# Group means of twelve chains by a round trip through DRAM and a sum on VectorE, in place of a product on TensorE

## The chip, the core and the metric

The kernel runs on one core of one Trainium2 chip. The metric is the time of one execution in microseconds (us) on the device; lower is better. The engines have short names in every row of the profile: PE is TensorE (PEld its weight loads), DVE is VectorE, ACT is ScalarE, POOL is GpSimd, SP is SyncE, which here only issues DMAs.

## What is computed

Sixteen images of 128 channels by 32x32 pixels pass through two convolution layers, each ahead of a group norm and with a residual sum. Cut to what matters:

```python
def _gn(v, G=32, eps=1e-05):          # 32 groups of 4 channels
    g = v.reshape(B_, G, C_ // G, H_, W_)
    m = jnp.mean(g, axis=(2, 3, 4), keepdims=True)
    s = jnp.var(g, axis=(2, 3, 4), keepdims=True)
    return ((g - m) / jnp.sqrt(s + eps)).reshape(v.shape)

def L0(x):                            # 4 experts, mixed per image
    routing = sigmoid(mean(x, (2, 3)) @ w_route.T + b_route)
    y = conv3x3(x, w_experts)         # 128 -> 4 * 128 channels
    out = einsum('beohw,be->bohw', y, routing)
    return silu(out * inv + shift)

x = x + L0(_gn(x))
x = x + conv3x3(_gn(x), sign(W))      # L1
```

The change concerns only the mean `m` of the two group norms: the mean over four neighbouring channels of the channels' own means.

## The kernel before

The 128 channels lie on the 128 partitions, and an image is a tile `X` of 128x1024. The kernel handles one image per **iteration** `t` of a software pipeline. In iteration `t` TensorE does the first convolution of image `t` (lines 439: `pb`, `pa`, `pe_`, with kernels `U`/`UM` mixed for this image by ACT line 704 and DVE line 932), then the second convolution of image `t-1` (line 474: a high and a low half, `hi` and `lo`, `pc<-hi,ws` and `pc<-lo,ws`, 18 products each). Each engine has its own written-out program; the order of its instructions is the order of the calls in the code, and semaphores are the only link between engines. Nothing is scheduled by a planner.

Group norms are done in **chains**, one chain `c` an iteration, `c = t + 2`. A chain handles two columns at once: column `IN`, the first norm of image `c`, and column `MID`, the second norm of image `c - LAG` (`LAG = 3`, so image `t-1`). The steps of a chain, with their lines:

- `nm[:, c, :]`, the two negated means of each channel, scaled: ACT line 584 (`mean_mid`, from the sum that the silu of line 732 leaves in `ysum`) and ACT line 572 (`mean_in`, `junk_mean<-X`, whose result is written by the READ_ACCUMULATOR after it).
- **the group means** `gnm`: PE line 405 (`group_means`), a product of `nm` (two columns) with the matrix `gsum`, into the PSUM bank `ps`.
- the squares of each channel's distance from its group's mean: ACT line 635 (`squares`, written to `dev2`; the profile shows it as `dev<-ps,nm`), `deviation` (line 651), `add_variance` (line 645, writes `spread`).
- the group variances: PE line 410 (`group_vars`), then ACT line 663 (`ve`), POOL line 352 (`power`, `rstd<-ve,nhalf`: the reciprocal root), ACT line 668 (`nbias`, reads `gnm` again), and ACT lines 747, 754, 686, which write `hi`, `hn` and `xn` from the normalised images.

Around this, within iteration `t` on VectorE: `all_rows(t+1)` (line 963, `e_rows`), `inner_rows(t+1)` (972, `f_rows`), `transform(t+1)` (980 to 990, `V`), one third of the mix of kernels for `t+1` (932), then the inverse transform of image `t` (997 to 1023, it waits for `pa` and ends in `y`), `low_part(t-1)` (1044, `lo<-hn,hi`), the rest of the mix with `pool_routes` (911) between, and the kernels' rows (941 to 955).

The residual sum of the first layer, `X<-y`, is an accumulating DMA of 512 KB issued by POOL (line 356) when silu is done; ACT line 592 (`junk_mid`) waits for it. SP issues the loads of `x` and, image by image as these residual sums land, the store of `X` to `out` (line 334, 512 KB):

```python
            for i in range(B - LATE):
                wait_h(sp, i)
                sp.dma_start(out_v[i, :, :], img(i)).then_inc(h_stored[i], 16)
```

POOL adds the second layer's result to `out` by another accumulating DMA (line 361), once that store is done.

Of the kernel before, what the change touches and what calls it, by code (L numbers as in the profile page):

```python
# [7 lines left out]
F32 = mybir.dt.float32  # L8
# [8 lines left out]
GSIZE = 4  # L17
# [39 lines left out]
def build(nc, x, w_experts, w_sign, params, out):  # L57
# [6 lines left out]
    with ExitStack() as ctx:  # L64
        def sb(name, shape, dt=F32):
            return ctx.enter_context(nc.sbuf_tensor(name, shape, dt))
# [4 lines left out]
        def sem(name):  # L71
            return ctx.enter_context(nc.semaphore(name))
# [46 lines left out]
        junk = {n: sb(f"junk_{n}", [C, HW]) for n in ("mean", "var", "mid")}  # L119
        warm_out = sb("warm_out", [C, 1])  # L120
# [42 lines left out]
        gnm_ready = sem("gnm_ready")  # L163
        dev_ready = sem("dev_ready")
# [43 lines left out]
        ND = 1  # L208
        DVE_RESIDUAL = (0, B - 1)
# [44 lines left out]

        def gnm(c, a, b):
            return small_bank(c)[:, 2 * c + a:2 * c + b]
# [55 lines left out]
        def _(sp):  # L312
# [16 lines left out]
            for i in range(4, B):  # L329
                sp.wait_ge(x_loaded[i - 3], 16)  # L330
                load(i)
            for i in range(B - LATE):
                wait_h(sp, i)
                sp.dma_start(out_v[i, :, :], img(i)).then_inc(h_stored[i], 16)
            done = 0
# [50 lines left out]
        def _(pe):  # L386
# [5 lines left out]

            def group_means(c):
                a, b = cols(c)
                if b > IN:
                    pe.wait_ge(nm_in_ready, c + 1)
                if a == MID:
                    pe.wait_ge(nm_mid_ready, c - LAG + 1)

                if c > 2:  # L400
                    wait(pe, nbias_mid_ready, c - LAG)
                    pe.wait_ge(nbias_in_ready, min(c, B))
                    pe.wait_ge(dev_ready, min(c, B))
                    pe.wait_ge(th_ready, min(c, B))
                mm_(gnm(c, a, b), gsum[:], nm[:, c, a:b], start=True, stop=True).then_inc(gnm_ready, 1)  # L405

            def group_vars(c):
                a, b = cols(c)
                pe.wait_ge(spread_ready, columns_to(c))
                mm_(gvar(c, a, b), gmat[:], spread[:, c, a:b], start=True, stop=True).then_inc(gvar_ready, 1)  # L410
# [155 lines left out]
        def _(act):  # L566
# [59 lines left out]
            def squares(c):  # L626

                a, b = cols(c)
                act.wait_ge(gnm_ready, c + 1)
# [209 lines left out]
        def _(dve):  # L839
# [67 lines left out]

            def pool_routes(c):
# [183 lines left out]
            for t in range(1, B):  # L1092

                all_rows(t + 1)
                if t == 1:
                    residual(0)
                inner_rows(t + 1)
# [42 lines left out]
```

## Time and profile before

| | |
|---|---|
| median of 3 runs | 281.71 us (279.56 to 281.97) |
| the profiled execution | 279.12 us, its span 277.3 us |
| PE busy | 270.6 us (98% of the span) |
| PEld busy | 185.7 us (67%) |
| DVE busy | 245.5 us (89%) |
| ACT busy | 208.5 us (75%) |
| POOL busy | 52.5 us (19%) |
| share of the chain that ended last | PE 88%, ACT 4%, DVE 3%, issue 1%, DMA 1% |
| DMA | 34.68 MB, mean 125 GB/s |

The span is the stretch of the profile from the first instruction to the last; the execution's own time is 1.8 us more. A time with two decimals, as 138.50, is a moment in us from the span's start. An image's iteration repeats with a period of 15.72 us, so one period stands for all in the rows below.

### The profile page before, as it was taken

How to read it: one execution, taken by the hardware profiler on the slowest of the kernel's cores; microseconds unless marked ns; L12 is line 12 of the kernel's file. 1: busy time of each engine (PE TensorE's matmuls, PEld its weight loads, DVE VectorE, ACT ScalarE, POOL GpSimd, SP SyncE). 2: the span in 40 equal slices, each digit the busy share in tenths (PEclk: the TensorE clock that was granted, in tenths of full speed). 3: DMA queues.
4: the chain of work that ended last, by engine and by line, in shares of the span. 5: the costliest groups of instructions: out<-in, count | busy, mean ns of one | idle time of the engine just before them, and what ended most of it. 6: DMA issues, size and time to landing. Idle time of an engine off the chain costs nothing.

```text
span 277.3 us, 4016 instructions
## 1 busy us (share of the span) xinstructions
PE 270.6 (98%) x1324; PEld 185.7 (67%) x1324; DVE 245.5 (89%) x439; ACT 208.5 (75%) x421; POOL 52.5 (19%) x59
## 2 busy tenths in 40 slices
PE   7999899999999999999999999999999999999996
PEld 6644756759586776859576775858576675848554
DVE  4898989999999999999999999999999999992732
ACT  3597788886988788787979788796978885727750
POOL 2001011214111031414123041414113041212000
PEclk9999999999999999999999999999999999999999
DMA  7999925442635445362635544371554545460422
GB/s 229 391 381 325 274 118 147 77 99 67 118 103 95 132 79 132 51 120 79 113 113 78 151 74 105 68 136 76 95 135 76 152 58 96 103 125 2 76 76 78
DMA packets 11397, 34.68 MB, mean 125 GB/s; under 512 B 1264, under 2 KB 3568, under 8 KB 11376
## 3 DMA queue, kind: packets, MB, share of 16 engines
q0 software_dynamic: 4032, 14.68, 31.3%
q1 hardware_dynamic: 7056, 19.47, 19.1%
q8 instruction: 11, 0.18, 0.3%
q10 hardware_dynamic: 288, 0.26, 0.3%
q14 instruction: 10, 0.08, 0.1%
HBM read 11.34 MB, written 15.73 MB: 98 GB/s over the span
## 4 chain that ended last, share of the span: by engine, by line
PE 88%; ACT 4%; DVE 3%; issue 1%; DMA 1%; POOL 1%; SPq 0%; ACTq 0%; DVEq 0%
PE pc L474 40%; PE pb L439 14%; PE pa L439 13%; PE pe_ L439 12%; PE pd L429 6%; DMA X<-x 1%; PE ps L410 1%; PE ps L405 1%; PE pb L474 1%; PE ps L414 1%; ACT y L738 1%; POOL rstd L352 1%; DVE U L932 0%; ACT hn L754 0%; DVE lo L1044 0%
## 5 line engine op out<-in xcount | busy, mean ns | idle before, releaser
L474 PE MATMUL pc<-lo,ws 128*128 128x496 f16 (+5 forms) x288 | 64.7, 371 | 0.0
L932 DVE SCALAR_TENSOR_TENSOR U<-we,route,U 128x1152 f32<-128x1152 f32 x45 | 63.5, 1410 | 0.1
L474 PE MATMUL pc<-hi,ws 128*128 128x496 f16 (+5 forms) x288 | 62.8, 372 | 0.0
L352 POOL TENSOR_TENSOR rstd<-ve,nhalf 128x2 f32<-128x2 f32 (+1 forms) x19 | 26.4, 1391 | 136.5 <-ACT ve L663 136.5
L474 PEld LDWEIGHTS pc<-hi,ws 128*128 128x128 f16 x288 | 28.1, 98 | 30.8 <-issue 0.3
L474 PEld LDWEIGHTS pc<-lo,ws 128*128 128x128 f16 x288 | 28.4, 105 | 25.5
L439 PE MATMUL pa<-V,UM 128*128 128x256 f32 (+1 forms) x180 | 41.8, 382 | 0.0
L439 PE MATMUL pb<-V,UM 128*128 128x256 f32 (+1 forms) x180 | 40.6, 375 | 0.1
L439 PE MATMUL pe_<-V,U 128*128 128x256 f32 (+1 forms) x180 | 40.6, 375 | 0.0
L439 PEld LDWEIGHTS pb<-V,UM 128*128 128x128 f32 x180 | 34.1, 190 | 5.7 <-issue 0.8
L439 PEld LDWEIGHTS pe_<-V,U 128*128 128x128 f32 x180 | 34.1, 190 | 3.8
L439 PEld LDWEIGHTS pa<-V,UM 128*128 128x128 f32 x180 | 33.1, 190 | 3.2
L592 ACT ACTIVATE junk_mid<-X,nm 128x1024 f32<-128x1024 f32 x15 | 17.3, 1151 | 15.2 <-DMA X<-y 15.2
L356 POOL DMA_DIRECT2D X<-y x14 | 12.3, 882 | 68.5 <-ACT y L732 68.5
L997 DVE TENSOR_TENSOR sums<-pa,minus 128x512 f32<-128x512 f32 x15 | 10.4, 691 | 12.9 <-PE pa L439 12.9
L747 ACT ACTIVATE hi<-X,nbias,rstd 128x1024 f16<-128x1024 f32 (+2 forms) x18 | 20.4, 1144 | 0.5
L1044 DVE TENSOR_TENSOR lo<-hn,hi 128x1024 f16<-128x1024 f32 x16 | 19.5, 1216 | 1.2 <-ACT hn L754 1.2
L754 ACT ACTIVATE hn<-X,nbias,rstd 128x1024 f32<-128x1024 f32 x16 | 19.7, 1228 | 0.0
L732 ACT ACTIVATE y<-y,bn_shift,bn_tiles 128x1024 f32<-128x1024 f32 x14 | 17.2, 1232 | 2.9 <-DVE y L1023 2.9
L686 ACT ACTIVATE xn<-X,nbias,rstd 128x1024 f32<-128x1024 f32 (+1 forms) x16 | 19.3, 1205 | 0.0
L704 ACT ACTIVATE U<-we,route 128x1152 f32<-128x1152 f32 x15 | 18.8, 1256 | 0.5
L668 ACT ACTIVATE nbias<-ps,rstd 128x1 f32<-128x1 f32 x30 | 7.6, 253 | 14.4 <-POOL rstd L352 14.4
(110 smaller groups left out, 387.2 us busy)
## 6 DMA issues: line engine op xcount, KB each, us to landing
X<-x SPq DMA_DIRECT2D x15, 512.0 KB, 5.2
out<-X SPq DMA_DIRECT2D x14, 512.0 KB, 2.6
X<-y POOLq DMA_DIRECT2D x14, 512.0 KB, 4.5
out<-ev POOLq DMA_DIRECT2D x14, 512.0 KB, 5.5
we<-w_experts SPq DMA_DIRECT2D x3, 768.0 KB, 8.2
out<-X SPq DMA_DIRECT2D x3, 256.0 KB, 2.0
ws_raw<-w_sign SPq DMA_DIRECT2D x1, 576.0 KB, 10.9
X<-x ACTq DMA_DIRECT2D x2, 128.0 KB, 3.0
```

The lines of the kernel that those rows point to most:

```text
L352: g.tensor_tensor(rstd[:, c, a:b], ve[:, c, a:b], nhalf[:, a:b], ALU.pow).then_inc(rstd_ready, 1)
L429: mm = mm_(rows[:, r0 - half * (H // 2):r1 - half * (H // 2), c0:c1], U[i % RING][:, slot, kx * C:(kx + 1) * C], xn[i % RING][:, r0 + ky:r ...
L439: mm = mm_(bank[:, :, j, c0:c1], weights[:, kx * C:(kx + 1) * C], V[t % 2][:, :, k, c0 + kx - 1:c1 + kx - 1], start=(n == 0), stop=(n == K ...
L474: mm = mm_(rows[:, r0 - first // W:r1 - first // W, c0:c1], ws[:, tap * C:(tap + 1) * C], (hi, lo)[part][i % 2][:, r0 + ky - 1:r1 + ky - 1 ...
L592: activation(junk["mid"][:], img(i), ACT.Square, bias=nm[:, c, MID:MID + 1], scale=1.0 / ROOT_HW, accum_out=var[:, c, MID:MID + 1]).then_i ...
L686: activation(xn[i % RING][:, 1 + first:1 + last, :], img(i).rearrange("p (h w) -> p h w", h=H)[:, first:last, :], ACT.Identity, bias=nbias ...
L704: activation(flat(U[i % RING][:]), flat(we[:, 0, :, :]), ACT.Copy, scale=route[:, i, 0:1]).then_inc(mix_first, 1)
L732: activation(flat3(y[i % 2][:]), flat3(y[i % 2][:]), ACT.Silu, bias=bn_shift[:, 0:1], scale=bn_tiles[:, 0:1], accum_out=ysum[:, i:i + 1]). ...
L747: activation(hi[i % 2][:, first:last, :], img(i).rearrange("p (h w) -> p h w", h=H)[:, first:last, :], ACT.Identity, bias=nbias[:, c, MID: ...
L754: activation(hn[:], img(i), ACT.Identity, bias=nbias[:, c, MID:MID + 1], scale=rstd[:, c, MID:MID + 1]).then_inc(hn_ready, 1)
L932: v.scalar_tensor_tensor(out=flat(U[i % RING][:]), in0=flat(we[:, e, :, :]), scalar=route[:, i, e:e + 1], in1=flat(U[i % RING][:]), op0=AL ...
L1044: v.tensor_tensor(flat(lo[i % 2][:]), hn[:], flat(hi[i % 2][:]), ALU.subtract).then_inc(lo_ready, 1)
```

## The change

Chains 4 to 15 (`DRAM_CHAINS = (LAG + 1, B)`, twelve of the nineteen) no longer use PE line 405. Instead SP writes the chain's 128x2 means from `nm` to a small array in DRAM, waits until they are there, and loads them back into `members`, in such a way that each partition gets the eight numbers of its group's four channels. DVE sums the four and scales the sum into `gmean` in SBUF. ACT's `squares`, `deviation` and `bias` read `gmean` where they read PSUM before. The other chains (0 to 3 and 16 to 18) stay as they were.

```diff
+        members = [sb(f"members{p}", [C, GSIZE, 2]) for p in range(2)]
+        member_sum = sb("member_sum", [C, CHAINS, 2])
+        gmean = sb("gmean", [C, CHAINS, 2])
+        means = nc.dram_tensor("means", (CHAINS, C, 2), F32, kind="Internal").ap()
...
+        DRAM_CHAINS = (LAG + 1, B)
...
+        def through_dram(c):
+            return DRAM_CHAINS[0] <= c < DRAM_CHAINS[1]
+        def through_dram_to(c):
+            return (c - DRAM_CHAINS[0]) // 2 + 1
         def gnm(c, a, b):
+            if through_dram(c):
+                return gmean[:, c, a:b]
             return small_bank(c)[:, 2 * c + a:2 * c + b]
...
+            def share_means(c):
+                if not through_dram(c):
+                    return
+                sp.wait_ge(nm_mid_ready, c - LAG + 1)
+                sp.wait_ge(nm_in_ready, c + 1)
+                sp.dma_start(means[c, :, :], nm[:, c, :]).then_inc(means_stored[c % 2], 16)
+                sp.wait_ge(means_stored[c % 2], 16 * through_dram_to(c))
+                wait(sp, member_sum_ready, c - 1 - DRAM_CHAINS[0])
+                of_group = means[c, :, :].rearrange("(g j) k -> g (j k)", j=GSIZE)
+                sp.dma_start(flat(members[c % 2][:]),
+                             of_group.unsqueeze(1).broadcast_to([C // GSIZE, GSIZE, 2 * GSIZE])) \
+                  .then_inc(members_loaded[c % 2], 16)
             for i in range(B - LATE):
                 wait_h(sp, i)
                 sp.dma_start(out_v[i, :, :], img(i)).then_inc(h_stored[i], 16)
+                share_means(i + LAG + 1)
...
             def group_means(c):
                 a, b = cols(c)
+                if through_dram(c):
+                    return
...
             def group_vars(c):
                 a, b = cols(c)
                 pe.wait_ge(spread_ready, columns_to(c))
+                if through_dram(c):
+                    bank_read(c)
...
             def squares(c):
-                act.wait_ge(gnm_ready, c + 1)
+                if through_dram(c):
+                    act.wait_ge(gmean_ready, c + 1 - DRAM_CHAINS[0])
+                else:
+                    act.wait_ge(gnm_ready, c + 1 if c < DRAM_CHAINS[0] else c + 1 - DRAM_CHAINS[1] + DRAM_CHAINS[0])
...
+            def sum_members(c):
+                if not through_dram(c):
+                    return
+                dve.wait_ge(members_loaded[c % 2], 16 * through_dram_to(c))
+                v.tensor_reduce(member_sum[:, c, :], members[c % 2][:].rearrange("p j k -> p k j"),
+                                axis=mybir.AxisListType.X, op=ALU.add).then_inc(member_sum_ready, 1)
+                dve.wait_ge(member_sum_ready, c + 1 - DRAM_CHAINS[0])
+                v.tensor_scalar(gmean[:, c, :], member_sum[:, c, :], ROOT_HW / GSIZE, None, ALU.mult) \
+                 .then_inc(gmean_ready, 1)
...
                 all_rows(t + 1)
                 if t == 1:
                     residual(0)
+                sum_members(t + LAG - 1)
                 inner_rows(t + 1)
```

`bank_read(c)` holds the four waits on the readers of the bank `ps` that `group_means` had: they move, for these chains, to `group_vars`.

TensorE, the low half of the second convolution in an iteration in the middle, before: the group-mean product stands between its two halves.

```order
L474 MATMUL pc<-lo,ws 128x512
L474 MATMUL pc<-lo,ws 128x16x31 x2
L405 MATMUL ps<-nm,gsum 128x2 [waits nbias_in_ready,dev_ready,nbias_mid_ready,th_ready,nm_mid_ready,nm_in_ready]
L474 MATMUL pc<-lo,ws 128x512 [waits lo_ready]
L474 MATMUL pc<-lo,ws 128x16x31 x2
```

The same place now (line 516 is the old 474):

```order
L516 MATMUL pc<-lo,ws 128x512
L516 MATMUL pc<-lo,ws 128x16x31 x2
L516 MATMUL pc<-lo,ws 128x512 [waits lo_ready]
L516 MATMUL pc<-lo,ws 128x16x31 x2
L516 MATMUL pc<-lo,ws 128x512
```

The product is gone, and the four waits on the bank's readers now stand at the group-variance product.

VectorE at the start of an iteration, before:

```order
L955 SCALAR_TENSOR_TENSOR UM<-U,even 128x384 [waits even_ready]
L963 SCALAR_TENSOR_TENSOR e_rows<-xn 128x1024 [waits xn_ready]
L972 TENSOR_TENSOR f_rows<-xn 128x512
L980 TENSOR_TENSOR V<-e_rows 128x8x32 [waits e_ready]
L983 SCALAR_TENSOR_TENSOR V<-f_rows 128x8x32 [waits f_ready]
```

And now:

```order
L1010 SCALAR_TENSOR_TENSOR UM<-U,even 128x384 [waits even_ready]
L1018 SCALAR_TENSOR_TENSOR e_rows<-xn 128x1024 [waits xn_ready]
L957 TENSOR_REDUCE member_sum<-members 128x2 [waits members_loaded1]
L960 TENSOR_SCALAR gmean<-member_sum 128x2 [waits member_sum_ready]
L1027 TENSOR_TENSOR f_rows<-xn 128x512
L1035 TENSOR_TENSOR V<-e_rows 128x8x32 [waits e_ready]
```

Two instructions stand between `e_rows` and `f_rows`, and the first waits for the load of `members`; all that follows on VectorE in the iteration is queued behind it.

SP's queue now, where there was one store an iteration (the first three rows are one iteration's):

```order
L368 DMA out<-X 128x1024 [waits added1]
L358 DMA means<-nm 128x2 [waits nm_in_ready,nm_mid_ready]
L362 DMA members<-means 128x1x8 [waits means_stored0]
L368 DMA out<-X 128x1024 [waits added0]
L358 DMA means<-nm 128x2 [waits nm_in_ready,nm_mid_ready]
```

The two small transfers stand between two stores.

## Rows read from the trace of the kernel before

**Rows 1.** The page: busy time; chain that ended last; then one period's busy times.
```profile
PE 270.6 (98%) x1324; PEld 185.7 (67%) x1324; DVE 245.5 (89%) x439; ACT 208.5 (75%) x421; POOL 52.5 (19%) x59
...
PE 88%; ACT 4%; DVE 3%; issue 1%; DMA 1%; POOL 1%; SPq 0%; ACTq 0%; DVEq 0%
...
134.46:150.18 15.72, 15.72 (x80) 10.99 (x78) 15.12 (x27) 13.02 (x27) 3.71 (x3) 1.00 0.47 99
```
**Rows 2.** Timeline of PE: start, duration, instruction; idle time before it in brackets.
```profile
138.50 0.28 PE L405 MATMUL ps<-nm,gsum 128*128 128x2 f32 x2
138.64 2.06 PE L474 MATMUL pc<-lo,ws 128*128 128x512 f16 x9
...
143.08 0.28 PE L410 MATMUL ps<-spread,gmat 128*128 128x2 f32 x2
```
**Rows 3.** Timeline of ACT, from one silu (L732) to the next.
```profile
134.46 1.23 ACT L732 ACTIVATE y<-y,bn_shift,bn_tiles 128x1024 f32<-128x1024 f32 x1
...
136.96 0.18 ACT L572 ACTIVATION_READ_ACCUMULATOR junk_mean<-X 128x1 f32 x1
...
140.66 1.15 ACT L592 ACTIVATE junk_mid<-X,nm 128x1024 f32<-128x1024 f32 x1 [0.80 <-DMA X<-y]
...
141.81 0.39 ACT L635 ACTIVATE dev<-ps,nm 128x1 f32<-128x1 f32 x2
...
143.28 0.60 ACT L721 ACTIVATE minus<-pb 128x512 f32<-128x512 f32 x1 [0.56 <-PE pb L439]
...
146.15 0.26 ACT L668 ACTIVATE nbias<-ps,rstd 128x1 f32<-128x1 f32 x1 [1.21 <-POOL rstd L352]
...
147.92 1.23 ACT L754 ACTIVATE hn<-X,nbias,rstd 128x1024 f32<-128x1024 f32 x1
...
150.18 1.23 ACT L732 ACTIVATE y<-y,bn_shift,bn_tiles 128x1024 f32<-128x1024 f32 x1
```
**Rows 4.** Timeline of DVE in the same iteration.
```profile
140.45 1.22 DVE L963 SCALAR_TENSOR_TENSOR e_rows<-xn 128x1024 f32<-128x1024 f32 x1
...
141.59 0.68 DVE L972 TENSOR_TENSOR f_rows<-xn 128x512 f32<-128x512 f32 x1
...
144.13 1.41 DVE L932 SCALAR_TENSOR_TENSOR U<-we,route,U 128x1152 f32<-128x1152 f32 x1
...
146.11 0.69 DVE L997 TENSOR_TENSOR sums<-pa,minus 128x512 f32<-128x512 f32 x1 [0.57 <-PE pa L439]
...
148.65 0.75 DVE L1023 SCALAR_TENSOR_TENSOR y<-pe_,outer 128x256 f32<-128x256 f32 x2
149.32 1.22 DVE L1044 TENSOR_TENSOR lo<-hn,hi 128x1024 f16<-128x1024 f32 x1
```
**Rows 5.** Timeline of DVE near the start: two small dependent instructions.
```profile
5.05 0.27 DVE L882 BATCH_NORM_AGGREGATE agg<-parts 128x2 f32<-128x24 f32 x1
5.34 0.15 DVE L884 TENSOR_SCALAR nm<-agg 128x1 f32<-128x1 f32 x1
```
**Rows 6.** Windows of 0.5 us: the share before GB/s is that of the DMA engines.
```profile
137.50:138.00 0.50, 0.50 (x4) 0.24 (x3) 0.47 (x2) 0.50 (x1) 0.00 (x0) 1.00 1.31 254
...
139.50:140.00 0.50, 0.50 (x4) 0.26 (x3) 0.50 (x3) 0.36 (x2) 0.00 (x0) 1.00 1.10 213
```
**Rows 7.** DMAs to landing: the parameters' load (KB, us); the last stores, of line 340.
```profile
prm<-params SPq DMA_DIRECT2D x1, 6.0 KB, 3.2
...
DMA to landing us min/median/max: 1.7/2.0/2.0
```
**Rows 8.** Line 352: all powers, ns min/median/max; then two of them, and a mix.
```profile
L352 POOL TENSOR_TENSOR rstd<-ve,nhalf x19: 548/2001/2007, 7.6 to 264.6; 128x2 f32<-128x2 f32 x13, 128x1 f32<-128x1 f32 x6
...
144.11 2.00 POOL L352 TENSOR_TENSOR rstd<-ve,nhalf 128x2 f32<-128x2 f32 x1 [7.16 <-ACT ve L663]
...
81.21 0.71 POOL L352 TENSOR_TENSOR rstd<-ve,nhalf 128x2 f32<-128x2 f32 x1 [7.16 <-ACT ve L663]
81.23 1.41 DVE L932 SCALAR_TENSOR_TENSOR U<-we,route,U 128x1152 f32<-128x1152 f32 x1
```

More of the change, by code:

```diff
@@ L163, in build @@
         gnm_ready = sem("gnm_ready")
+        means_stored = [sem("means_stored0"), sem("means_stored1")]
+        members_loaded = [sem("members_loaded0"), sem("members_loaded1")]
+        member_sum_ready = sem("member_sum_ready")
+        gmean_ready = sem("gmean_ready")
         dev_ready = sem("dev_ready")
@@ L391, in warm, with bank_read @@
                     mm_(pd[:, 0, 0:C], ones[:], ones[:], start=True, stop=True)
+            def bank_read(c):
+                wait(pe, nbias_mid_ready, c - LAG)
+                pe.wait_ge(nbias_in_ready, min(c, B))
+                pe.wait_ge(dev_ready, min(c, B))
+                pe.wait_ge(th_ready, min(c, B))
             def group_means(c):
                 a, b = cols(c)
+                if through_dram(c):
+                    return
                 if b > IN:
@@ L400, in group_means @@
                 if c > 2:
[L401 to L404, printed above, removed]
+                    bank_read(c)
                 mm_(gnm(c, a, b), gsum[:], nm[:, c, a:b], start=True, stop=True).then_inc(gnm_ready, 1)
@@ L409, in group_vars @@
                 pe.wait_ge(spread_ready, columns_to(c))
+                if through_dram(c):
+                    bank_read(c)
                 mm_(gvar(c, a, b), gmat[:], spread[:, c, a:b], start=True, stop=True).then_inc(gvar_ready, 1)
```

## The prediction, made before the changed kernel had run

> **What bounds the kernel now.** I read the page's busy times and the chain that ended last first, then one iteration as a timeline, engine by engine. PE is busy 98% of the span and makes up 88% of the chain [rows 1]. In the period from the silu at 134.46 to the next at 150.18, which is 15.72 us, PE is busy all of it, at a granted clock of 1.00; DVE is busy 15.12 us and ACT 13.02 us [rows 1]. So TensorE sets the period, and nothing else does. But the others are close, and what matters here is how much each has left.
>
> - DVE waits once an iteration, 0.57 us for `pa` ahead of line 997 [rows 4].
> - ACT waits three times: 0.80 us for the residual's DMA, 0.56 us for `pb`, 1.21 us for POOL's power [rows 3]. The first of these lies just ahead of the squares that read the group means.
> - Around all engines runs a loop: silu, the means of the channels, the group means, squares, variance, power, `hi`, `hn`, `xn`, next silu. In this loop the group means lie ready long before their use. `mean_in` is written at 136.96 + 0.18 = 137.14, the product runs at 138.50, the squares start at 141.81 [rows 2, 3]. Between 137.14 and 141.81 there are 4.67 us, and this is where the change puts its round trip.
>
> **What it removes.** One product of two columns an iteration on TensorE (two passes). From its start to the next product's start are 138.64 - 138.50 = 0.14 us [rows 2], all on the path that sets the end. Twelve times that is 1.7 us, 0.6% of the time; more cannot be gained. PE's period becomes 15.72 - 0.14 = 15.58 us. The four waits that move to the variance product are for instructions of the iteration before, long done.
>
> **What it adds on VectorE.** A reduce of 128x8 to 128x2 and a scaling of 128x2 that waits for it. No reduce is in the trace. The nearest pair is a small aggregate and a scaling that waits for it, 5.34 - 5.05 = 0.29 us from start to start, and 0.15 us for the second [rows 5]. The lower bound is two instructions of 0.15 us without a gap, 0.3; the upper is 0.29 + 0.15 = 0.44. The next instruction starts some 0.08 us before the end of the one ahead of it (141.59 against 140.45 + 1.22 = 141.67 [rows 4]), so I take 0.35 us. DVE then has 15.12 + 0.35 = 15.47 us of work, still under PE's 15.58 and hidden by the 0.57 us of wait.
>
> If the load is in time, the reduce starts at 141.60, `gmean` is there at 142.0, and the squares start at 142.05 and not at 141.81. These 0.24 us on ACT are covered by its 0.56 us of wait for `pb` [rows 3]; PE, which reaches the variance product at 143.08 [rows 2] and with the product gone 0.14 earlier, may wait up to 0.05 us for `spread`. I take 0.03 us of that. The period of the twelve iterations would be 15.61 us, and the sum 12 x (15.61 - 15.72) = -1.3 us.
>
> **What it adds in DMAs.** Call L the moment at which `members` has landed. SP sees `nm` at about 137.2 and issues the write. Neither such a small store nor such a small load is in the trace. A store of 128 to 256 KB on a quiet machine lands in 1.7 to 2.0 us, which bounds the write from below at 1.7; the only small load, 6 KB at the start among other loads, took 3.2 us, the upper bound [rows 7]. Here the write is not alone. The residual's accumulating DMA was issued at the same silu, and the DMA engines are fully busy with it from 137.5 to 140.0 [rows 6]. If the write's 128 pieces stand in line with it, it lands when that one is through, near 140.3, which is 3.1 us; if not, in 1.7. I take 2.6. The read is issued when the residual is nearly over, ahead of the store of `X`, and I take 2.0 for it, out of 1.7 to 3.2. With 0.1 us for each hand-over L = 137.2 + 2.6 + 0.1 + 2.0 + 0.1 = 142.0; its bounds are 140.8 and 143.8.
>
> The Trainium skill (DMA: Bandwidth & Descriptors, Anatomy of one DMA) gives, fitted on DMAs that GpSimd issues, a fixed cost of about 2.0 us for each, most of it the wait until the last byte is confirmed, with HBM as the slowest target. By that L would be 137.2 + 4.2 = 141.4, and the sum the same -1.3 us. The same page (Queues, rings and completion order) says that a DMA engine takes turns between its queues, packet by packet, which speaks for the later landing.
>
> DVE reaches the reduce at 141.6, so from L = 141.6 on it stands and waits, and queued behind the reduce are `f_rows`, `V`, the mix, the inverse transform and so the next silu. How late may L be? The loop is: silu to L, then 0.4 for the sum, then on DVE from `f_rows` to the end of the mix 145.54 - 141.59 = 3.95, the inverse transform 149.40 - 146.11 = 3.29, and 0.1 to silu [rows 4]. Counted from silu at 134.46 [rows 3], the period is L - 134.46 + 7.74 us. It meets 15.61 at L = 142.3. So L = 142.0 still costs nothing, with 0.3 us to spare; every 0.1 us beyond 142.3 costs 1.2 us in all.
>
> SP's queue: the store of `X` stands behind the read. It goes out as the residual lands, at about 140.6 [rows 3], and would now go out some 0.3 us later at L = 142.0; POOL issues its user, the second accumulating DMA, only behind the power, at 146.1 [rows 8], 5 us later. This costs nothing.
>
> **POOL's power.** It takes 2.00 us at 144.11, and 0.71 us at 81.21 [rows 8]. The mix on DVE starts 0.02 us behind it both times (144.13 and 81.23), and in the long cases the power ends 0.57 us after the mix ends (146.11 against 145.54 [rows 4, 8]). So the two exclude each other, and it is a matter of some ten nanoseconds who comes first. The change moves the mix 0.35 us or more later against the power, which now comes in the middle of the `V` instructions ahead of it. I expect it to be let in at the next boundary between two DVE instructions, as at 81.21, and to end about 1 us earlier than it does today; ACT has then 1 us more to spare, and the loop above, not the one through ACT, is the one that counts.
>
> The Trainium skill (SBUF — State Buffer, Who interferes with whom) names this: a VectorE instruction with two SBUF inputs contends with a GpSimd one that reads SBUF, and whichever started first blocks the other for the whole instruction. By that the power waits for one `V` instruction of 0.4 to 0.7 us, not for the mix, and the sum is my -1.3 us. The trace has no power that arrives amid such a row of short instructions.
>
> **Rival 1: the round trip is late.** The mechanism is the loop above with L beyond 142.3: VectorE stands at the reduce, and TensorE then stands at the variance product. For it speaks that the write leaves into DMA engines that are full for 2.5 us [rows 6] and that the only small load took 3.2 us [rows 7]; against it, that 4.67 us are there for two transfers whose floor is 1.7 each. At L = 143.2 the period is 143.2 - 134.46 + 7.74 = 16.48, and the sum 12 x 0.76 = +9 us; at the upper bound of 143.8, 17.08 and +16 us. It decides from L = 142.3 on. Its time is about 291 us, from 282 to 298.
>
> **Rival 2: the power is shut out.** If VectorE never lets go between back-to-back instructions, the power still ends 0.57 us after the mix, and the mix is later by all that the sum costs. Then there is a second loop: `f_rows` 141.59, mix, power, `hn` ending at 147.92 + 1.23 = 149.15, and `lo` on DVE, which can start at 149.20 and today starts at 149.32 [rows 3, 4]; from there to the next `f_rows` at 157.31 are 7.99 us. That is 7.61 + 7.99 = 15.60 us today, just below the period, and 15.95 with the 0.35 us added: 12 x 0.23 = +3 us even with L in time. And a late L goes through it too: silu, L, 0.4, then 150.18 - 141.59 = 8.59 to silu. At L = 142.0 that is 7.54 + 0.4 + 8.59 = 16.53 us a period, +10 us. It decides from L = 141.2. For it: the median of the nineteen powers is 2.00 us [rows 8]. Against it: at 81.21 the power got in between `V` and mix, which follow each other without a gap. Its time is 285 to 292 us.
>
> **How the numbers follow.** The sum is made against the profiled execution: 279.12 - 1.3 = 277.8 us. The median of the runs shown is 281.71, which is 2.6 us above it for a reason that the trace does not show; I set the prediction against the median, 281.71 - 1.3 = 280.4 us. A change under 1% can hardly be told from none on this kernel, whose three runs span 0.9%. Chances: my forecast 0.47, with its own range 277.5 to 282.5; rival 1 0.26; rival 2 0.20; something I have not seen 0.07, either way. From these, faster by over 1% 0.05 (the sum has no room for it, only the spread of the runs has), within 1% 0.50 (the forecast, and the mildest edges of the rivals), slower 0.45. The range from 277.5 to 293 leaves out rival 1 above L = 143.4 and rival 2 with such an L, about 0.15, and some 0.05 below.
>
> **What the profile will show.** If I am right: no line 405 product between the `lo` halves in the middle, a period near 15.6 us, PE without waits over 0.1 us, the load of `members` landing under 4.9 us after `nm`, a short or no wait of DVE at the reduce, and powers of 0.7 to 1.4 us. If rival 1 is: the reduce waits 0.7 us or more for the DMA, and PE waits for `spread` each time. If rival 2 is: powers of 2 us or more that end 0.57 us after the mix, with ACT's `nbias` waiting for them. The prediction is wrong above all if two small transfers take over 5 us together beside the residual's.

## The result, and the profile of the changed kernel

The changed kernel takes 335.91 us (median of 4 runs, 335.61 to 337.28), the kernel before 280.64 us beside it (4 runs, 279.56 to 281.97). The ratio is 1.2002, with a 95% interval from 1.1946 to 1.2058: slower by 55 us. I had forecast 280.4 us, with a range from 277.5 to 293. A few executions of a kernel come out over 1.5% above its fastest (in experiment 9 two of four), and the ratios here and below are formed without them.

The page of the changed kernel, in the order of [rows 1]: span (its mean granted clock is 0.939), busy times, two rows of the forty slices, the chain that ended last by engine and by line, and four groups of instructions.

```profile
span 333.8 us, 4026 instructions
...
PE 292.2 (88%) x1300; PEld 196.0 (59%) x1300; DVE 249.5 (75%) x463; ACT 214.3 (64%) x421; POOL 47.3 (14%) x59
...
PE   7999887969789697997959979699796978999996
...
PEclk9999997989979799797998979989798997999999
...
PE 36%; DMA 30%; ACT 15%; DVE 12%; issue 5%; SPq 1%; POOL 0%; DVEq 0%; ACTq 0%
DMA means<-nm 19%; PE pa L481 17%; DMA members<-means 9%; PE pc L516 7%; ACT y L777 5%; PE pd L471 5%; ACT junk_mean L614 4%; PE pe_ L481 2%; PE pb L481 2%; DVE sums L1052 2%; DMA we<-w_experts 2%; DVE y L1078 2%; DVE diffs L1053 2%; ACT spread L690 2%; PE ps L452 2%
...
L481 PE MATMUL pa<-V,UM 128*128 128x256 f32 (+1 forms) x180 | 61.5, 514 | 0.0
...
L452 PE MATMUL ps<-spread,gmat 128*128 128x2 f32 (+1 forms) x34 | 6.5, 259 | 35.7 <-ACT spread L690 35.5
...
L1052 DVE TENSOR_TENSOR sums<-pa,minus 128x512 f32<-128x512 f32 x15 | 10.4, 692 | 31.0 <-PE pa L481 31.0
...
L957 DVE TENSOR_REDUCE member_sum<-members 128x2 f32<-128x8 f32 x12 | 1.9, 161 | 33.9 <-DMA members<-means 33.9
```

And its view of DMAs, the two new ones: times issued, KB, median us to landing.

```profile
means<-nm SPq DMA_DIRECT2D x12, 1.0 KB, 5.2
members<-means SPq DMA_DIRECT2D x12, 4.0 KB, 2.6
```

PE was busy 98% of the span and made up 88% of the chain [rows 1]; now it is 88% and 36%, and 30% of the chain are DMAs: 19% the write of the means, 9% the read. Three waits answer to that. DVE stands 33.9 us at the reduce for the load, 12 times. PE stands 35.5 us at the variance product for `spread`. DVE stands another 31.0 us for `pa`. Most of the third has its cause in line 481: these products take 514 ns each, though they are the same products as before, where they took 382, and the clock row has sevens and eights where nines should be.

The mean period from silu to silu over the twelve iterations is 20.38 us (19.99 to 21.00), where it was 15.72 [rows 1]. 12 x 4.66 = 55.9 us, and the span is 56.5 us longer: all but 0.6 us of it lies in these iterations.

One of them as the chain of waits gives it, start and duration of each piece, from one silu to the next. Its write is the slowest of the twelve.

```profile
161.06 1.34 ACT y L777 x2
...
163.84 6.49 DMA means<-nm
...
170.34 2.05 DMA members<-means
...
172.42 0.17 DVE member_sum L957
...
172.82 0.03 ACT dev L680
...
173.91 0.38 PE ps L452 x2
174.29 4.34 PE pa L481 x12
...
178.73 0.69 DVE sums L1052
...
182.06 1.24 ACT y L777
```

The path that now sets the period, stretch by stretch, this period's numbers beside it: silu to the issue of the write 2.78 us, the write 6.49, the read 2.05, reduce to squares 172.82 - 172.42 = 0.40, squares to the variance product 1.09, from there to `sums` 4.82, `sums` to silu 3.33. Before, the same stretch from the variance product to `sums` took 146.11 - 143.08 = 3.03 us [rows 2, 4]. Most of the other 1.79 us is the clock. Windows of 0.5 us around PE's wait: busy time of PE, PEld, DVE, ACT and POOL, granted clock, DMA share and GB/s.

```profile
171.00:171.50 0.50, 0.00 (x0) 0.00 (x0) 0.00 (x0) 0.00 (x0) 0.00 (x0) 1.00 0.00 0
173.50:174.00 0.50, 0.09 (x1) 0.09 (x1) 0.50 (x3) 0.50 (x3) 0.00 (x0) 1.00 0.00 0
...
174.50:175.00 0.50, 0.50 (x4) 0.46 (x3) 0.50 (x2) 0.50 (x2) 0.33 (x1) 0.92 0.00 0
175.00:175.50 0.50, 0.50 (x3) 0.43 (x2) 0.50 (x2) 0.50 (x1) 0.50 (x1) 0.50 0.00 0
...
178.50:179.00 0.50, 0.50 (x4) 0.45 (x3) 0.27 (x1) 0.50 (x2) 0.00 (x0) 1.00 0.87 172
```

PE has nothing to do for 3.45 us, until 173.91. The granted clock stays at 1.00 (2.4 GHz) through the gap, falls to 0.50 (1.2 GHz) at 174.92 (the window's 0.92 puts it there), 1.0 us after PE has begun again and 0.6 us into `pa`, and is back before 178.5. Most of `pa`, the very products that `sums` waits for, runs in those 3.4 us. The same happens in all twelve iterations, after waits of PE of 2.4 to 3.45 us; the clock falls 0.1 to 1.5 us after PE has begun again.

So the sum over an average period is: the reduce begins 10.71 us after silu (issue 2.80, write 5.30, read 2.57 and hand-overs), and from there to the next silu are 0.40 + 1.09 + 4.82 + 3.36 = 9.67 us: 20.38 us. In experiment 4, where the clock stays at 1.00, the 4.82 us are 3.13; so 1.69 us are the clock, and 0.10 of the 1.79 is there without it. Against the forecast's 15.61 the late round trip is 3.08 us and the clock 1.69. Whether each of these stretches is cause and not company is what the experiments are for.

### The profile page after: what moved, and what is told of

It is laid out like the page before. It is cut to its first block, busy times and chain, and to the rows that moved or that the text cites. A ratio compares the mean times of both kernels' runs of the same rounds, so it can differ in the third digit from the quotient of the medians.

```text
span 333.8 us, 4026 instructions
## 1 busy us (share of the span) xinstructions
PE 292.2 (88%) x1300; PEld 196.0 (59%) x1300; DVE 249.5 (75%) x463; ACT 214.3 (64%) x421; POOL 47.3 (14%) x59
## 4 chain that ended last, share of the span: by engine, by line
PE 36%; DMA 30%; ACT 15%; DVE 12%; issue 5%; SPq 1%; POOL 0%; DVEq 0%; ACTq 0%
DMA means<-nm 19%; PE pa L481 17%; DMA members<-means 9%; PE pc L516 7%; ACT y L777 5%; PE pd L471 5%; ACT junk_mean L614 4%; PE pe_ L481 2%; PE pb L481 2%; DVE sums L1052 2%; DMA we<-w_experts 2%; DVE y L1078 2%; DVE diffs L1053 2%; ACT spread L690 2%; PE ps L452 2%
## 5 line engine op out<-in xcount | busy, mean ns | idle before, releaser
L516 PE MATMUL pc<-lo,ws 128*128 128x496 f16 (+5 forms) x288 | 63.1, 372 | 0.0
L481 PE MATMUL pa<-V,UM 128*128 128x256 f32 (+1 forms) x180 | 61.5, 514 | 0.0
L481 PEld LDWEIGHTS pa<-V,UM 128*128 128x128 f32 x180 | 46.6, 266 | 8.5
L387 POOL TENSOR_TENSOR rstd<-ve,nhalf 128x2 f32<-128x2 f32 (+1 forms) x19 | 20.7, 1092 | 175.7 <-ACT ve L708 175.7
L452 PE MATMUL ps<-spread,gmat 128*128 128x2 f32 (+1 forms) x34 | 6.5, 259 | 35.7 <-ACT spread L690 35.5
L481 PEld LDWEIGHTS pe_<-V,U 128*128 128x128 f32 x180 | 35.0, 195 | 4.3
L680 ACT ACTIVATE dev<-gmean,nm 128x1 f32<-128x1 f32 x24 | 5.8, 287 | 41.1 <-DVE gmean L960 41.1
L452 PEld LDWEIGHTS ps<-spread,gmat 128*128 128x128 f32 x34 | 5.4, 193 | 41.4 <-ACT spread L690 40.8
L957 DVE TENSOR_REDUCE member_sum<-members 128x2 f32<-128x8 f32 x12 | 1.9, 161 | 33.9 <-DMA members<-means 33.9
```

The source lines that it names most:

```text
L387: g.tensor_tensor(rstd[:, c, a:b], ve[:, c, a:b], nhalf[:, a:b], ALU.pow).then_inc(rstd_ready, 1)
L481: mm = mm_(bank[:, :, j, c0:c1], weights[:, kx * C:(kx + 1) * C], V[t % 2][:, :, k, c0 + kx - 1:c1 + kx - 1], start=(n == 0), stop=(n == K ...
L516: mm = mm_(rows[:, r0 - first // W:r1 - first // W, c0:c1], ws[:, tap * C:(tap + 1) * C], (hi, lo)[part][i % 2][:, r0 + ky - 1:r1 + ky - 1 ...
```

## Experiments

The first four ran beside 23 runs of the kernel before (median 279.46 us), the next four beside 17 (279.49), the last three beside 23 (280.39).

**1. Side DMAs in the kernel before.** The group means stay on TensorE, and SP sends copies of the change's transfers with nobody waiting for them but SP: 8 bytes a partition to DRAM and the read back, the same to SBUF, 512 bytes a partition to DRAM, and 8 bytes to DRAM once the residual has landed.

```
             for i in range(B - LATE):
                 wait_h(sp, i)
+                share_means(i + LAG, True)
                 sp.dma_start(out_v[i, :, :], img(i)).then_inc(h_stored[i], 16)
+                share_means(i + LAG + 1, False)
...
+                if c % 4 == 0:
+                    side_dma(w8_dram[c, :, :], nm[:, c, :])
...
+                    side_dma(w8_sbuf[:, c, :], nm[:, c, :])
...
+                    side_dma(w512_dram[c, :, :], gsum[:])
...
+                    side_dma(w8_late[c, :, :], nm[:, c, :])
```

> The kernel of before with its product on TensorE, and beside it, once an iteration for chains 4 to 15, a DMA of SP for whose data nobody waits; only SP itself waits for the landing. Four kinds, three of each: 8 bytes a partition from nm to DRAM at the moment of the changed kernel (and read back), the same to SBUF, 512 bytes a partition to DRAM, and 8 bytes to DRAM but only once the residual's DMA has landed. In the changed kernel the first kind took 5.2 us. Theory A (the write stands in line with the residual's accumulating DMA): the first, the second and the third take about 5 us, the late one 1.7 to 2.2 us. Theory B (8-byte pieces into DRAM are slow by themselves): the first and the late one take about 5 us, the one to SBUF 2 and the one of 512 bytes at most 3. Under both the time of the kernel stays within 1% of before, 279 to 283 us, since nothing waits.

Its time is 279.73 us, ratio 1.0017 (0.9988 to 1.0047): the transfers by themselves cost nothing. Their rows in the view of DMAs, columns as above:

```profile
w_dram<-gsum SPq DMA_DIRECT2D x3, 64.0 KB, 3.6
w_dram<-nm SPq DMA_DIRECT2D x3, 1.0 KB, 5.0
r_sbuf<-w_dram SPq DMA_DIRECT2D x3, 4.0 KB, 2.6
w_sbuf<-nm SPq DMA_DIRECT2D x3, 1.0 KB, 3.6
w_late<-nm SPq DMA_DIRECT2D x3, 1.0 KB, 3.0
```

The write takes 5.0 us with nobody behind it, so it isn't slow for anything that the kernel does in return. Neither theory alone explains it. Beside the residual every write takes at least 3.6 us, also 8 bytes to SBUF and 512 bytes to DRAM. The packets of the trace show why. In the changed kernel the write is issued at 163.84, its first packet runs at 166.74, and the residual's last one ends at 166.92; the late write of this experiment, with the residual gone, has its first packet 0.82 us after the issue. So the small write gets no turn until the residual is nearly through. And the 8-byte pieces to DRAM take 1.4 us more on top, and are the slow ones again when the residual is gone (3.0).

**2. The change without its DMAs.** The reduce reads the channel's own mean eight times in place of the eight members, so the group means are left out.

```
-                share_means(i + LAG + 1)
...
-                dve.wait_ge(members_loaded[c % 2], 16 * through_dram_to(c))
-                v.tensor_reduce(member_sum[:, c, :], members[c % 2][:].rearrange("p j k -> p k j"),
+                dve.wait_ge(nm_mid_ready, c - LAG + 1)
+                dve.wait_ge(nm_in_ready, c + 1)
+                v.tensor_reduce(member_sum[:, c, :], nm[:, c, :].unsqueeze(2).broadcast_to([C, 2, GSIZE]),
```

> The changed kernel without its two small DMAs: VectorE sums each channel's own mean four times over instead of the four members of the group, so the group means of the twelve chains are left out of the computation. All else stays: no product on TensorE, the two instructions on VectorE, gmean read by ScalarE. Theory: the whole loss hangs on the round trip, and the rest of my sum holds: 1.3 us faster than before, 278 to 281 us. Rival (the power on GpSimd is shut out behind the mix and the second loop binds): 3 us slower than before, 283 to 284 us, with powers of 2 us or more and ScalarE waiting for them each time.

It takes 282.03 us, ratio 1.0071 (1.0044 to 1.0097): almost all of the 55 us goes with the DMAs, but it isn't the gain of 1.3 us that I had for a round trip in time. Every period is 15.82 us, not 15.61. The timelines of DVE and of ACT show why, with the engine's idle time before the instruction in brackets:

```profile
144.23 0.15 DVE L957 TENSOR_REDUCE member_sum<-nm 128x2 f32<-128x8 f32 x1
...
148.85 0.69 DVE L1052 TENSOR_TENSOR sums<-pa,minus 128x512 f32<-128x512 f32 x1 [0.39 <-PE pa L480]
...
160.05 0.15 DVE L957 TENSOR_REDUCE member_sum<-nm 128x2 f32<-128x8 f32 x1
```

```profile
144.62 0.48 ACT L679 ACTIVATE dev<-gmean,nm 128x1 f32<-128x1 f32 x2 [0.81 <-DVE gmean L960]
```

From `sums` to the next reduce DVE works without a gap, 160.05 - 148.85 = 11.20 us, as it did up to `f_rows` before (157.31 - 146.11, [rows 4] and the prediction). From the reduce the path leaves DVE: 0.39 us to the squares on ACT, 1.09 to the variance product (145.71), 3.14 to `sums`, 4.62 in all. 11.20 + 4.62 = 15.82. This loop didn't exist before, because the group means didn't come from DVE. The instructions themselves are as sized: 0.15 and 0.17 us, 0.27 from the reduce's start (144.23) to that of `f_rows` (144.50).

**3. The residual held back until the write has landed.**

```
                 pool.wait_ge(silu_ready, silus(i))
+                if through_dram(i + LAG):
+                    pool.wait_ge(means_stored[(i + LAG) % 2], 16 * through_dram_to(i + LAG))
                 g.dma_start(img(i), flat3(y[i % 2][:]), accum_op=ALU.add).then_inc(added[i % 2], 16)
```

> The changed kernel, but GpSimd issues the residual's DMA only when the write of the means has landed, so that the write has the DMA engines to itself. Theory A (the write stands in line with the residual): the write takes 1.7 to 2.2 us instead of 5.2; the residual lands some 3 us later than now, so the squares start about 1 us a period earlier, and the time is about 325 us. Theory B (8-byte pieces into DRAM are slow): the write still takes 5 us, the residual lands after it, and the time is about 360 us.

The write falls from 5.2 to 2.8 us (median), so 2.4 us of it were the residual. It does not fall to 1.7: there is a second part, the same as in experiment 1. The time is 358.46 us (one run), for the residual is now the late one. From the timeline, in one iteration:

```profile
204.95 0.16 DVE L959 TENSOR_REDUCE member_sum<-members 128x2 f32<-128x8 f32 x1 [1.15 <-DMA members<-means]
...
207.24 1.15 ACT L636 ACTIVATE junk_mid<-X,nm 128x1024 f32<-128x1024 f32 x1 [5.50 <-DMA X<-y]
...
209.46 0.59 PE L454 MATMUL ps<-spread,gmat 128*128 128x2 f32 x2 [4.22 <-ACT spread L692]
209.91 5.36 PE L483 MATMUL pa<-V,UM 128*128 128x256 f32 x12
```

The squares stand behind `junk_mid`, which needs the residual's sum. And PE's longer gap, 4.22 us, is followed by a `pa` of 5.36 us, where the gap of 3.45 us was followed by 4.34. Here the granted clock is down before PE begins again, as a window in the columns of above shows:

```profile
208.50:209.00 0.50, 0.00 (x0) 0.00 (x0) 0.50 (x1) 0.50 (x4) 0.00 (x0) 0.50 0.98 401
```

**4. PE kept busy through the wait.** Ten products whose result nobody reads, ahead of the variance product; nothing else is changed.

```
+                        if through_dram(c):
+                            warm(10)
                         group_vars(c)
```

> The changed kernel with ten products of ones (as in the warm-up at the start) on TensorE ahead of each variance product of the twelve chains, into a bank that nobody reads any more; they take about 2.5 us of the 2.4 to 3.5 us for which TensorE stands there. Theory: of the 4.6 us that a period has grown, 1.7 are not the wait itself but the clock behind it: the granted clock falls to the lower level 1 us after the wait and pa takes 4.47 us instead of 2.78. Then the clock stays at 1.00, pa takes 2.8 us and the time falls by about 12 x 1.7 = 20 us, to 316 us. Rival (pa is slow for another reason, or the loop runs through ScalarE and not through pa): the time stays at 334 to 338 us.

315.12 us, ratio 1.1245 (1.1195 to 1.1296), clock 1.0 in the whole span. PE's longest wait for `spread` is 1.2 us, and `pa` is back at 382 ns a product. From the variance product to `sums` it is now 3.13 us:

```profile
165.42 0.38 PE L452 MATMUL ps<-spread,gmat 128*128 128x2 f32 x2 [1.21 <-ACT spread L692]
...
168.55 0.69 DVE L1054 TENSOR_TENSOR sums<-pa,minus 128x512 f32<-128x512 f32 x1 [0.39 <-PE pa L481]
```

The mean period is 18.52 us: 1.69 less by the clock, and 0.18 by a reduce that begins a little earlier, 10.53 us after silu. Work was added and 20.8 us were gained: the clock's share is shown.

**5. The variance product behind `pa`.** The same aim with no work added: PE does `pa` first, which needs nothing from the group means.

```
-                    else:
+                    elif not through_dram(c):
                         group_vars(c)
                     plus_points(t)
-                    if t == 1:
+                    if t == 1 or through_dram(c):
                         group_vars(c)
```

> The changed kernel, but for the twelve chains TensorE runs the variance product (line 452) behind the products of pa instead of ahead of them, so that it has 2.7 us of work in its wait. Theory (a period is: silu, means, write, read, sum, squares, variance product, pa at the low clock, inverse transform on VectorE, silu): pa drops out of the loop, its clock stays at 1.00, and what is left runs through the power and ScalarE, some 2 us a period shorter; the time is about 312 us. Rival (VectorE stands at its reduce, and everything behind that is what counts): the time stays within 2% of 336 us.

312.26 us, ratio 1.1185 (1.1124 to 1.1245), clock 1.0, mean period 18.45. The write still takes 5.1 us. The chain of waits no longer goes through `pa`. It goes through the power, `nbias`, `hn` and `xn`, and from the reduce to silu are 7.62 us where experiment 4 has 7.95, so some 4 of the 23.6 us gained are this shorter path and not the clock. What remains after either cure of the clock is the late round trip, 32 to 34 us.

**6. The mean of the input ahead of silu on ACT**, so that `nm` is there earlier and the write is issued together with the residual, not 1.1 us behind it.

```
                     normalise(c)
+                if c + 1 < B:
+                    mean_in(c + 1)
                 silu(t)
...
-                if c + 1 < B:
-                    mean_in(c + 1)
```

> The changed kernel, but ScalarE runs mean_in of the next image ahead of the silu instead of behind it, where it waits 1.9 us a period for y anyway. The write of the means can then leave 1.1 us earlier against the silu. Theory (the round trip lies wholly in the loop): 12 x 1.1 = 13 us less, about 323 us. Rival (the write ends when the residual's DMA lets it, whenever it is issued): the write takes 1.1 us longer instead, and the time stays at about 336 us.

I was wrong by 35 us: 288.22 us, ratio 1.0322 (1.0262 to 1.0383). I had moved the write earlier and kept its duration, but the duration fell too, to 3.0 us. In one iteration it is issued at 157.31, the residual at 157.26. The write's packets run from 158.13 to 158.32, the residual's begin at 158.70: the few bytes are out before. The landing is early enough for PE to wait 1.5 us at the most, and the clock stays at 1.0.

**7. Experiment 2 with the sum at another place**, ahead of the rows of the forward transform on DVE. The group means are left out as there.

```
+                sum_members(t + LAG - 1)
                 all_rows(t + 1)
...
-                sum_members(t + LAG - 1)
                 inner_rows(t + 1)
```

> The kernel without the two small DMAs (each channel's own mean is summed four times, the group means of twelve chains are left out), but VectorE does its two small instructions ahead of e_rows instead of behind it. With them behind e_rows it was 0.7% slower than before. Theory: a loop binds that I had left out, from VectorE's sum through ScalarE's squares to the variance product, pa and back to VectorE; here the group means are ready 1.2 us earlier, the loop is open, and the kernel is 1.3 us faster than before, 278 us. Rival (the two instructions on VectorE or the reads of SBUF by ScalarE cost the time wherever they stand): it stays 2 us slower than before, 281 to 282 us.

279.35 us, ratio 0.9965 (0.9933 to 0.9997), profiled execution 277.52; all periods in the middle are 15.59 us. This opens the loop of experiment 2, and what is left is PE's own work, my 15.58. So the product on TensorE costs what I said, and all that its removal can give here is about a third of a per cent.

**8. Side DMAs once the residual has landed**, in the kernel before, with one new kind: 8 bytes a partition to DRAM, 512 bytes apart.

```
+                if not SIDE[0] <= c < SIDE[1] or not late:
+                    return
...
+                if c % 4 == 3:
+                    side_dma(w8_apart[c, :, 0:2], nm[:, c, :])
```

> The kernel of before with its product on TensorE, and one DMA of SP an iteration beside it for whose data nobody waits, all now issued only when the residual's DMA has landed, ahead of the store of X. Four kinds, three of each: 8 bytes a partition to DRAM (and read back), the same to SBUF, 512 bytes a partition to DRAM, and 8 bytes a partition to DRAM with a pitch of 512 bytes. Before, the first kind took 2.7 to 3.1 us there. Theory C (small pieces that share lines of DRAM are slow): the first 2.9 us, the other three 1.7 to 2.1. Theory D (8-byte pieces into DRAM are slow wherever they go): the first and the pitched one 2.9, the one to SBUF and the one of 512 bytes 1.7 to 2.1. Theory E (some 2.9 us is the price of any small DMA of 128 pieces): all four 2.6 to 3.0.

```profile
w_dram<-gsum SPq DMA_DIRECT2D x3, 64.0 KB, 1.5
w_dram<-nm SPq DMA_DIRECT2D x3, 1.0 KB, 2.8
r_sbuf<-w_dram SPq DMA_DIRECT2D x3, 4.0 KB, 3.1
w_sbuf<-nm SPq DMA_DIRECT2D x3, 1.0 KB, 1.7
w_apart<-nm SPq DMA_DIRECT2D x3, 1.0 KB, 1.4
```

The time is 279.75 us (one run). It is neither the smallness of a piece nor DRAM: the same 8 bytes land in 1.4 us when they lie 512 bytes apart, 512-byte pieces land in 1.5, and only the packed ones, side by side in one kilobyte, take 2.8. The packets of both run from 0.82 to 1.02 us after the issue. The ones that lie apart have landed 0.38 us after the last packet, the packed ones 1.7 to 2.1 us after it: the time is lost between the last packet and the landing.

The Trainium skill (DMA: Bandwidth & Descriptors, Anatomy of one DMA) has about 2.0 us for the fixed cost of one that GpSimd issues. Issued by SP here, the cheapest is 1.4 us, below that figure, and the packed write is above it.

**9. The changed kernel with its groups 512 bytes apart in DRAM.** The eight members of a group still lie together, so that the read is as before.

```
-        means = nc.dram_tensor("means", (CHAINS, C, 2), F32, kind="Internal").ap()
+        means = nc.dram_tensor("means", (CHAINS, C // GSIZE, C), F32, kind="Internal").ap()
...
-                sp.dma_start(means[c, :, :], nm[:, c, :]).then_inc(means_stored[c % 2], 16)
+                sp.dma_start(means[c, :, 0:2 * GSIZE].rearrange("g (j k) -> g j k", j=GSIZE), nm[:, c, :]).then_inc(means_stored[c % 2], 16)
...
-                of_group = means[c, :, :].rearrange("(g j) k -> g (j k)", j=GSIZE)
+                of_group = means[c, :, 0:2 * GSIZE]
```

> The changed kernel, but in the array in DRAM the groups lie 512 bytes apart, so that the 8-byte pieces of different groups no longer lie beside each other (the four of one group still do). On a quiet machine 8-byte pieces took 2.8 us packed and 1.4 us when each stood 512 bytes from the next. Theory (what is slow is pieces of different groups in one line of DRAM; the residual holds back the rest): the write beside the residual takes 3.6 us, like the ones to SBUF and of 512 bytes, not 5.3; each period is 1.6 us shorter by that alone, 317 us, and if TensorE's wait gets short enough for its clock to stay at the upper level, up to 1.7 us a period more, 297 us. Rival (all pieces of one line must be apart): no change, 336 us.

292.74 us (4 runs: 289.36, 290.52, 294.95, 296.42), ratio 1.033 (1.0245 to 1.0415). The two DMAs:

```profile
means<-nm SPq DMA_DIRECT2D x12, 1.0 KB, 3.7
members<-means SPq DMA_DIRECT2D x12, 4.0 KB, 2.0
```

The write loses 1.5 us of its 5.2 and keeps the 3.7 that it spends beside the residual. PE's waits for `spread` fall to 10.8 us in all, 1.6 at the longest, the clock stays (0.999 in the profiled execution; the two longer runs have 0.994 and 0.988, so there it did not stay up throughout), `pa` takes 382 ns a product, and the mean period is 16.63 us. That is 3.75 us less than in the changed kernel: 1.69 of the clock, and 2.06 of a reduce that begins earlier by that much. The layout alone gives back 45 of the 55 us (profiled executions, 335.61 and 290.52), and 20 of them are not its own but the clock's.

**10. Experiments 6 and 9 together.**

> The groups 512 bytes apart in DRAM, and mean_in ahead of the silu as in the run that came out at 288 us. Theory: the write leaves before the residual's bytes flow and takes 1.5 us instead of 3.0; the means are then there before VectorE comes to its reduce, and the kernel comes to where the one without DMAs and with the sum behind e_rows stood, a period of 15.82 us, 281 to 282 us. Rival (the read, now beside the residual, takes over what the write has given back): 285 to 288 us.

282.42 us (12 runs, 281.70 to 285.28), ratio 1.0068 (1.0033 to 1.0103): the best version that still makes the round trip. Its two DMAs:

```profile
means<-nm SPq DMA_DIRECT2D x12, 1.0 KB, 2.0
members<-means SPq DMA_DIRECT2D x12, 4.0 KB, 2.6
```

The reduce waits once in twelve times, 0.5 us, and most periods are 15.82 us, those of experiment 2. With both transfers in time only the loop through DVE is left.

**11. Experiment 10 with the sum at the place of experiment 7.**

> As the one before (groups apart, mean_in ahead of the silu), and VectorE does its sum ahead of e_rows, 1.2 us earlier. Theory: members lands 1.7 + 1.5 + 0.1 + 2.6 = 5.9 us after the silu's start, just before VectorE reaches the place at 6.0, so that the loop of 15.82 us is open too and the kernel is as fast as the one without DMAs and with the early sum, a period of 15.59 us and 278 to 279 us, 0.3% faster than before. Rival (the read is slower beside the residual): VectorE stands at the reduce, ahead of all its work for the next image, and the kernel is slower than the one before it, 284 us or more.

282.51 us (12 runs, 281.44 to 283.92), ratio 1.0076 (1.0043 to 1.0110), so nothing gained, and neither expectation met. The periods alternate between 15.25 and 16.28 us in the middle, mean 15.82. In one of two the reduce, now ahead of `e_rows` on DVE, waits for its load, mostly some 0.5 us, in the next it doesn't. The wait shown is the longest in the middle, for a read that took 4.24 us:

```profile
160.93 0.16 DVE L957 TENSOR_REDUCE member_sum<-members 128x2 f32<-128x8 f32 x1 [1.15 <-DMA members<-means]
...
176.55 0.15 DVE L957 TENSOR_REDUCE member_sum<-members 128x2 f32<-128x8 f32 x1
```

Ahead of `e_rows` the sum comes too early for the transfers, behind it it closes the loop. The write and the read now take 4.7 us together, and the residual sets when they end: in experiments 10 and 11 the read, issued while the residual flows, lands 0.2 to 0.3 us behind it each time, as a rule 6.3 to 6.4 us after silu, where I had counted on 5.9. No version with the DMAs beats the kernel before.

## Why the prediction was wrong, step by step

**The removed product: right.** 0.14 us an iteration. Experiment 7, where nothing else is in the way, has 15.59 us a period against 15.58.

**DVE's two instructions: right in size, wrong in what hangs on them.** I had taken 0.35 us against 0.27 (from start to start) to 0.32 (both durations) measured, and had gone through ACT's wait and PE's wait one by one, with up to 0.05 us for PE. But a wait of PE for `spread` isn't one that a period absorbs. It feeds back through `pa` and `sums` to the next reduce, and that loop is 15.82 us long. The step was "the period of the twelve iterations would be 15.61 us". This is worth 0.7% (experiment 2), and the forecast would have been wrong in its sign even had L been 142.0.

**The write: the step that failed.** "I take 2.6", with bounds of 1.7 and 3.2. It is 5.30 us on average. Two parts, each shown by itself, make it up: some 3.6 us because it goes out only when the residual is nearly through (experiment 1; held back, the write falls by 2.4 us, experiment 3), and 1.4 to 1.6 us because the 128 pieces of 8 bytes lie packed in DRAM (experiments 8 and 9). I had thought of the first, put it at 3.1, and then took less than that, a value between this and 1.7. The second is in no row of the kernel before, and my upper bound for it came from a load of 6 KB at the start, a transfer of another direction, piece size and layout. A row of another kind was no bound.

**The read: within its bounds.** 2.0 to 2.9 us, for which I took 2.0 out of 1.7 to 3.2. So L was not 142.0 but 145.2 on average, counted from a silu at 134.46, beyond my bound of 143.8. The line "wrong above all if two small transfers take over 5 us together" names what came: they take 7.9.

**The loop from L to the next silu: right in size, on the wrong engine.** I had 7.74 us along DVE. DVE's own work from the reduce to silu is 4.22 + 3.33 = 7.55 us (172.42 to the mix's end at 176.64, and `sums` to silu); with the clock up the path is 7.95 us (experiment 4), along PE: squares, variance product, `pa`, `sums`. Both run side by side, and DVE waits 0.39 us for `pa`. Rival 1 had this mechanism and the right place, and at the measured L its formula gives 10.69 + 7.74 = 18.43 us a period, and 280.6 + 12 x 2.71 = 313 us, close to what experiments 4 and 5 show with the clock cured. I had given it 282 to 298 us.

**The clock: missing.** In none of my cases does a wait of PE cost more than itself. After 2.4 to 3.45 us without work PE ran 3.4 us at 1.2 GHz, mostly on the products that the path waits for, 1.69 us a period and 20 us in all (experiment 4: 20.8 us less). No row of the kernel before has a gap of PE over 1 us in the middle of the run, so its price could not be read there; that it has a price could have been an open term.

**The power: right, rival 2 wrong.** The prediction has rival 2 decide from L = 141.2 on; against the period of 15.61 us, which it uses elsewhere, it is 141.1, and nothing hangs on it. From the timeline of the changed kernel, the last `V` instruction, the power and the mix:

```profile
174.63 0.69 DVE L1045 TENSOR_TENSOR V<-e_rows 128x512 f32<-128x512 f32 x1
174.68 1.22 POOL L387 TENSOR_TENSOR rstd<-ve,nhalf 128x2 f32<-128x2 f32 x1 [11.11 <-ACT ve L708]
175.23 1.41 DVE L987 SCALAR_TENSOR_TENSOR U<-we,route,U 128x1152 f32<-128x1152 f32 x1
```

The power ends at 175.90, 0.58 us after `V` ends, though the mix has begun by then; before, it ended 0.57 us after the mix [rows 4, 8]. It was let in at the boundary, and all twelve powers are like it: 1.09 to 1.22 us. By the rule of the Trainium skill (SBUF — State Buffer, Who interferes with whom) that whichever started first blocks the other for one instruction, the trace agrees on the side of GpSimd. It doesn't show DVE blocked in turn: the mix beside the power's end took its usual 1.41 us.

**The store behind the read** is held up with SP, and nobody waits for it: no engine has a wait on it in the changed kernel. Right.

## What to carry to other kernels

Before a small DMA is put into a loop, measure it as a side transfer in the kernel before, with the same piece size, layout and neighbours: nobody waits for it, it costs nothing, and it would have given the 5 us here. When a source of a value moves to another engine, follow the new path all the way round to its own start; a wait that is small on each engine can close a loop that is longer than the period. And treat a wait on TensorE of some microseconds (here 2.4 and more) as dearer than itself.

## What the runs showed of the hardware that I had not expected

- Where small pieces lie in DRAM decides: 128 pieces of 8 bytes land in 2.8 us packed in 1 KB, in 1.4 us at 512 bytes apart, in 1.7 us in SBUF; 128 pieces of 512 bytes in 1.5 us. Why packed pieces are slow, the runs don't show.
- A small write issued 1.1 us after the issue of a 512 KB accumulating DMA of GpSimd runs its first packet 2.9 us later, when that one's last packets run, and lands 3.6 us after its issue; one issued within 0.05 us of it is hardly held up (3.0 us packed, 2.0 apart). The read takes 1.9 to 4.2 us; in experiments 10 and 11 it is the residual that holds it up, and elsewhere the cause of the spread is left open.
- TensorE's granted clock fell in all twelve iterations of the changed kernel, after gaps of 2.4 to 3.45 us and 0.1 to 1.5 us into the work that follows, and in all twelve of experiment 3, with gaps of 3.4 to 5.5 us, in six of them before PE had begun again. In the profiled executions of experiments 4 to 6 and 9 to 11, with gaps of up to 1.6 us, it did not fall in these iterations.
- Between the last packet of a small write and its landing lie 0.38 us when its 8-byte pieces are 512 bytes apart in DRAM, and 1.7 to 2.1 us when they are packed (experiment 8); in the changed kernel up to 3.4 us (163.84: last packet 166.96, landing 170.33).
